# First layer of a graph network on one core: number row and angles in PSUM, both node sums in one bank, three queue orders changed

## The reference

```
rel_t = node_vec[src] - edge_weight
enc   = cos(rel_t * time_w + time_b)                 # 32 per edge
e     = concat(enc, edge_attr_64) @ We               # 96 -> 128
k, v  = (x@Wk+bk)[src] + e, (x@Wv+bv)[src] + e ;  q = (x@Wq+bq)[dst]
alpha = sum(q*k per head) / 8
a     = softmax of alpha over the edges of one dst
h     = layernorm(x + segment_sum(v*a, dst) + x@Wskip + bskip)
out   = layernorm(h + segment_sum(edge_weight*h[src], dst) @ W.T + b)   # second layer
```

## Time and profile before

| | us |
|---|---|
| median of 3 runs | 9845.34 (9844.81 to 9847.26) |
| profiled execution | 9864.48 |
| its span | 9862.8 |

### The profile page before, as it was taken

The page is one execution under the profiler, slowest core; times in us unless marked ns, Lnnn a source line. Parts: engine busy times, 40 slices in busy tenths (PEclk is TensorE's granted clock), DMA queues, the critical chain, the costliest instruction groups (busy, mean ns, idle before and its releaser), DMA issues.

```text
span 9862.8 us, 272152 instructions
## 1 busy us (share of the span) xinstructions
PE 7624.6 (77%) x52868; PEld 7101.3 (72%) x52869; DVE 8560.3 (87%) x21301; ACT 5115.0 (52%) x20838; POOL 6708.6 (68%) x6871
## 2 busy tenths in 40 slices
PE   6477777777777777777756777788888888888855
PEld 2477777777777777777756777787888877877754
DVE  5899999999999999999987666799999999999968
ACT  2377777777777777777753333333333333333300
POOL 0477777777777777777745777777777777777720
PEclk8688988888888888898875555688888888888888
DMA  6467666676666666666632222355555555555544
GB/s 191 114 180 178 179 177 177 178 179 178 176 177 180 177 176 177 178 181 177 177 97 69 71 71 71 106 151 147 149 147 149 148 148 149 148 148 149 148 133 116
DMA packets 1631706, 1484.67 MB, mean 151 GB/s; under 512 B 792007, under 2 KB 1363043, under 8 KB 1631203
## 3 DMA queue, kind: packets, MB, share of 16 engines
q1 hardware_dynamic: 1374244, 848.34, 34.3%
q0 software_dynamic: 257088, 632.95, 22.8%
HBM read 1225.51 MB, written 254.87 MB: 150 GB/s over the span
## 4 chain that ended last, share of the span: by engine, by line
issue 25%; DVE 19%; POOL 18%; PE 14%; DMA 7%; ACT 7%; DVEq 6%; SPq 3%; ACTq 2%; POOLq 0%
POOL message_scratch L869 17%; DMA message_scratch<-ohT,idx 6%; PE bank L982 3%; DVE y_all L1537 3%; PE bank L973 3%; ACT arena L1154 2%; DVEq L531 2%; PE bank L955 2%; PE bank L1015 2%; PE bank L963 2%; DVE acc L1670 1%; SPq L728 1%; DVE oh L1583 1%; DVE oh L1576 1%; DVE kve L1523 1%
## 5 line engine op out<-in xcount | busy, mean ns | idle before, releaser
L817 POOL DMA_INDIRECT kv<-kv_scratch,arena x3136 | 3265.7, 1041 | 1236.6 <-issue 837.5
L869 POOL DMA_INDIRECT message_scratch<-ohT,idx x3232 | 3214.2, 994 | 1079.0 <-issue 880.2
L1261 ACT ACTIVATE ohT<-bank,kv 128x128 f32<-128x128 f32 x3232 | 923.9, 369 | 2703.8 <-DMA message_scratch<-ohT,idx 2665.1
L1154 ACT ACTIVATE arena<-arena,weights 128x65 f32<-128x65 f32 x7040 | 1771.6, 337 | 2.4 <-PE bank L982 2.3
L1063 PE MATMUL bank<-acc,oh 128*128 x6464 | 1211.2, 345 | 520.3 <-ACT ohT L1262 514.4
L1063 PEld LDWEIGHTS bank<-acc,oh 128*128 128x128 f32 x6464 | 1054.7, 247 | 627.7 <-issue 625.2
L1077 PE MATMUL bank<-oh,kve 128*128 128x128 f32 x8640 | 1387.7, 321 | 144.7 <-DVE arena L1838 107.8
L982 PE MATMUL bank<-arena,oh 128*128 128x130 f32 x7040 | 1164.1, 318 | 280.8 <-DVE acc L1670 274.8
L1077 PEld LDWEIGHTS bank<-oh,kve 128*128 128x128 f32 x8640 | 1248.0, 227 | 167.8 <-issue 157.3
L982 PEld LDWEIGHTS bank<-arena,oh 128*128 128x128 f32 x7040 | 1048.2, 227 | 362.6 <-issue 295.1
L973 PE MATMUL bank<-arena,ohT 128*128 128x128 f32 x7040 | 1090.6, 306 | 0.0
(11 more groups left out here) (232 smaller groups left out, 12653.6 us busy)
## 6 DMA issues: line engine op xcount, KB each, us to landing
kve<-message_scratch SPq DMA_DIRECT2D x2160, 129.0 KB
kve<-nodes_scratch SPq DMA_DIRECT2D x880, 256.0 KB
feat<-in_edge_attr_dram SPq DMA_DIRECT2D x880, 96.0 KB
feat<-block_scratch SPq DMA_DIRECT2D x812, 98.0 KB
arena<-q_scratch SPq DMA_DIRECT2D x880, 64.0 KB
message_scratch<-ohT,idx POOLq DMA_INDIRECT x3232
kv<-kv_scratch,arena POOLq DMA_INDIRECT x3136
feat<-in_edge_attr_dram SPq DMA_DIRECT2D x880, 32.0 KB
```

Source lines behind the costliest of these rows:

```text
L817: pool.indirect_dma_start(kv[:, k, g, :], None, kv_d, bass.IndirectOffsetOnAxis(ap=group_rows[:, half, k * G + g, 0:1].bitcast(I32), axis= ...
L869: pool.indirect_dma_start(msg_d, bass.IndirectOffsetOnAxis(ap=idx[:, k, g:g + 1], axis=0), sum_ring[:, k % RING1, g, :], None).then_inc(s_ ...
L1154: op = act.activation(wv[:, st.k % 2, g, h, :], vR[:, st.k, g, h, :], ACT.Copy, scale=weights[:, st.k // ROUND, g, st.k % ROUND, h:h + 1])
L1261: act.activation(sum_ring[:, st.k % RING1, g, 0:C], banks[2 + st.k % 2][:, g * P:(g + 1) * P], ACT.Copy, scale=taken[:, st.k, g, 2:3])
```

## The change

- `agg_ps`: both node sums lie in bank 6, one beside the other. PE's `sum_stage` waits for `s_acc` of the step just before (it waited for that of two steps before).
- Bank 7 holds the number row, time_b and `turns`. DVE's L1503, L1506, L1508 and L1559 read or write them there. Two copies fill them once.
- PE's order in a body: feat, q, e, sum (it was feat, sum, q, e).
- ACT's order: arg first, of step k+17 (it was behind sine, of step k+18); then featc, weigh, sine, and the once-a-round stages. `EDGES` follows.
- DVE's order: the block number before ke; `sum_stage` behind ke and angle(2); `forward_stage` behind onehotT and `backward_stage` behind product.

```
-        turns = room(BATCH * G * TD).rearrange("p (b t) -> p b t", t=TD)
-        agg_ps = [banks[6 + j][:, 0:HEADS * HB] for j in range(2)]
+        agg_ps = [banks[6][:, j * HEADS * HB:(j + 1) * HEADS * HB] for j in range(2)]
+        brow_ps = banks[7][:, P:P + TD]
+        turns = banks[7][:, 2 * P:2 * P + BATCH * G * TD].rearrange("p (b t) -> p b t", t=TD)
 # PE sum_stage
-                wait(pe, s_acc, st.before(2))
+                wait(pe, s_acc, st.s)
 # PE body
-  at(i, k, (feat_stage, 15), (sum_stage, 1), (q_stage, 14), (e_stage, 15))
+  at(i, k, (feat_stage, 15), (q_stage, 14), (e_stage, 15), (sum_stage, 1))
 # ACT body
-            EDGES, group1 = {0: 6, 6: 8, 14: 2}, {}
+            EDGES, group1 = {0: 7, 7: 8, 15: 1}, {}
-  at(i, k, (featc_stage, 15), (weigh_stage, 2), *sines, (arg_stage, 18), *gaps, *exps, *smalls)
+  at(i, k, (arg_stage, 17), (featc_stage, 15), (weigh_stage, 2), *sines, *gaps, *exps, *smalls)
 # DVE, once, ahead of the pipeline
+            dve.tensor_copy(irow_ps, irow[:, :])
+            dve.tensor_copy(brow_ps, brow[:, :]).then_inc(s_tab, 1)
+            dve.wait_ge(s_tab, 3)
 # DVE angle(0): brow -> brow_ps; onehot_stage: irow -> irow_ps
 # DVE body
-  at(i, k, *turn[0], (ve_stage, 14), *turn[1], (ke_stage, 14), *turn[2], (block_stage, 0), *once(5, forward_stage),
-     (onehotT_stage, 15), *once(5, backward_stage), (product_stage, 13), *once(4, run_stage, first_stage),
+  at(i, k, *turn[0], (ve_stage, 14), *turn[1], (block_stage, 0), (ke_stage, 14), *turn[2], (sum_stage, 0),
+     (onehotT_stage, 15), *once(5, forward_stage), (product_stage, 13), *once(5, backward_stage), *once(4, run_stage, first_stage),
      ...
-     (sum_stage, 0), *once(8, pen_stage), *once(2, keep_part(0), keep_part(1), keep_part(2)))
+     *once(8, pen_stage), *once(2, keep_part(0), keep_part(1), keep_part(2)))
```

More of the change, by code:

```diff
@@ L1212, in body @@
                     if k in EDGES:
-                        groups_stage(mybir.EngineType.Activation, group1, Step(i, k + 18), EDGES[k])
+                        groups_stage(mybir.EngineType.Activation, group1, Step(i, k + 17), EDGES[k])
                     sines = [(sine_stage, 16)] if k % BATCH == 0 else []
@@ L1502, in stage_of @@
                     if n == 0:
-                        op = dve.tensor_tensor(a, a, brow[:, :].unsqueeze(1).to_broadcast([P, BATCH * G, TD]), ALU.add)
+                        op = dve.tensor_tensor(a, a, brow_ps.unsqueeze(1).to_broadcast([P, BATCH * G, TD]), ALU.add)
                     elif n == 1:
@@ L1558, in onehot_stage @@
                 wait(dve, s_agg, st.before(QS))
-                dve.tensor_tensor(oh[:, st.k % QS, :, :], irow[:, :].unsqueeze(1).to_broadcast([P, G, P]),
+                dve.tensor_tensor(oh[:, st.k % QS, :, :], irow_ps.unsqueeze(1).to_broadcast([P, G, P]),
                                   rel0[:, st.k // ROUND, st.k % ROUND, :].unsqueeze(2).to_broadcast([P, G, P]), ALU.is_equal).then_inc(s_oh, 1)
```

## The result

The changed kernel took 10321.9 us (median of 4 runs, 10305.9 to 10334.1) against 9846.3 us for the kernel before, now also over 4 runs: a ratio of 1.0478, 95% interval 1.0462 to 1.0493. It is slower by 476 us; I forecast slower by 320 us, with 10305 us as the upper end of the range. The profiled execution took 10305.9 us, its span is 10304.2 us.

What follows compares the result with a forecast made beforehand. DVE bounds the kernel, though not quite, waiting for ACT's products and PE's e. Terms 2.12 - 0.90 - 0.23 + 1.40 + 0.52 = +2.91 us a round, times 110 rounds: +320 us, 10165 us; range 9985 to 10305.

Steps and rivals of the forecast that it cites:

- ACT's new order: Body 6: table load, exp and dropx now precede ACT's products, which angle(0) awaits without slack; +1.74 us a round.
- "Cost 0" for the wait of PE's sum: PE's sum waiting for the sum just before is covered by ACT's idle time; 0, range -0.2 to +0.4 us a round.
- The write into PSUM: DVE's L1506 loses its fast mode with a PSUM destination: 130 ns, four times a round, +0.52 us.
- Reads from PSUM: DVE's L1559, L1503 and L1508 cost nothing more with a PSUM operand; range -0.01 to +0.08 us per instruction.
- Rival 2: PSUM reads cost DVE 0.08 us in each of 16 instructions a round: 141 us on top, 10305 us; chance 0.07.
- -0.90 for e: PE makes e before the node sum, so ve's waits for PE fall away: -0.90 us a round.
- +2.12 in body 6: DVE's angle(0) waits longer for ACT's products: 1.74 from exp plus 0.38 from DVE's earlier node sum, per round.
- +1.40 in body 4: Later backward scan delays PE's small results, ACT's copy and the products behind it; angle(0) waits +1.40 us a round.
- +0.38 for the node sum in front of new: DVE's node sum now precedes new, so the chain to body 6's products begins 0.38 us later.
- The small copy: In body 4 ACT's smallc, about 0.2 us, stands before the products and waits for PE; part of +1.40 us a round.
- Rival 1: Only the exp delay counts, body 4's backward-chain delay being taken up: 166 us more, 10010 us; chance 0.15.
- Rival 3: Faster: ACT runs a body ahead, PE's early e wins, only 0.52 us is paid: 9778 us; chance 0.08.

Runs made afterwards that it cites:

- the extra work: The changed kernel with PE forming two of the eight node sums of a round (steps 3 and 5) twice over, same result: 10223.8 us, ratio 1.0377.

## Why the prediction was right in kind and wrong in size

*ACT's new order* was the right cause. Undoing it gives back all (9847.5 us); alone it costs 208 us. Exp in front of the products with no slack, +1.74 us: the rows after show 1.75 us.

*"Cost 0" for the wait of PE's sum* held: two banks change nothing (10274.3 and 10269.5 us). *The write into PSUM*, 0.52 us a round or 57 us, measured 52. *Reads from PSUM*, 0: held. Rival 2 (reads from PSUM cost DVE) has fallen with that.

*-0.90 for e* held in the wait, and PE's order alone is worth even more in the kernel before, 143 us.

*The terms that were mis-sized: the two waits behind PE, in body 6 and in body 4.* The forecast had +2.12 in body 6, less 0.68 of ve, so +1.44; measured is +1.95. It had +1.40 in body 4; measured is +1.89. The step that failed is that I took PE's part of both chains as unchanged: I added only what ACT and DVE put in between, and took PE as ready when the backward scan ends.

The chains by their parts, means over all rounds of the stretch. From new_stage's start to angle(0) of body 6 it took 6.55 us before and takes 8.81 after: +2.26, where I had +1.74 for exp. Feat starts 2.12 us after new_stage's start before and 2.46 after, +0.34. ACT's copy starts behind feat's start 0.06 later than before. From the start of weigh to that of the products it took 1.92 us and takes 3.78: exp makes 1.75 of it, and the table load starts 2.03 us after weigh where the products started 1.92 after it, 0.11. In body 4 PE's small products start 1.60 us after the backward scan's start, 1.26 before, again +0.34; another 0.2 us is issue time between copy and products.

The two 0.34 are PE's clock. PE stands 9.0 us a round before (630 us in 70 rounds) and 11.5 after (737 in 64), and more of its work then runs at the granted 0.50. From newT's start to feat's the clock was 0.50 throughout in 22 of 70 rounds before, in 52 of 64 after, and in 5 of 65 with the extra work. The round of the earlier trace rows was one of the slow ones (newT 1.89 us; the fast ones have 1.06), so the rows of a single round could not tell how many there are. From alphaT's start to the small products' the mean clock is 1.00 before, 0.82 after, 0.97 with the extra work. The wait just in front does not tell it: PE stood 1.67 us before alphaT in the kernel before and stands 0.82 after. With the extra work feat starts 1.96 us after new and the small products 1.28 us after the scan's start, and the kernel gets 98 us faster, more than the two 0.34 (75 us). Some of this loss, then, the kernel before pays as well.

In sum, of the 156 us that the forecast lacked, the two delays on PE are 2 x 0.34 x 110 = 75 us, the issue time behind the copy 22, the 0.06 and 0.11 of body 6 19, L1654 (353 ns in place of the 188 of before) 18, body 0 (0.28 where I had 0.15) 14. The first is shown by runs, the others are only read from rows, and some 8 us stay open.

*+0.38 for the node sum in front of new* is not settled. With DVE's order alone body 6 waits less than before (1.34 us for 1.87). With PE's new order in place it waits more: 1.52 us in the changed kernel with ACT's old order, 0.68 with PE's order alone. The place of the node sum was not taken back by itself in the changed kernel.

*The small copy* was priced too low for the same reason: 361 us alone in the changed surroundings (I expected 175 to 210). PE's small products are late there, body 4 waits for them, and in all 65 rounds of the stretch newT then runs at the granted 0.50, so body 6 waits longer too.

*Terms don't add.* From the kernel before, ACT +208, DVE +65, write +52, PE -143 add up to +182; together they make +476. The surplus comes with ACT's order. Without its term the sum is -26 us, and the kernel without it has 9847.5 us, where the kernel before had 9844.0. ACT's order costs 208 us alone and 474 in the changed surroundings. There the small products start 1.71 us after the backward scan's start even with ACT's old order, yet body 4 waits 0, since the products stand in front of the copy. Behind the copy the same lateness is on the path. The scans' new places are 79 us of it.

*Rival 1* (body 4's delay is absorbed) is refuted: 1.89 us a round there. *Rival 3* (faster) has half a truth: in the kernel before, PE's order alone wins 143 us.

## What to carry to other kernels

Rotating a cyclic queue is free only if no once-in-a-while stage changes sides; look which stages pass each other, and whether the consumer of the delayed one has slack in that body. Read an engine's durations at the clock it will have after the change: where an added wait makes PE stand longer, take the slow rows of the trace for the upper end, and count over many rounds how often they come in place of reading one. The largest gain lay in none of the edits of waits or memory, but in two moves of PE's queue: nothing that waits for a late result in front of work that others wait for.

## What the runs showed of the hardware that I had not expected

A second, useless forming of two node sums per round made the kernel 98 and 173 us faster, with the granted clock going from 0.87 to 0.90 and from 0.85 to 0.93 in the stretch of 3000 us. And a small DVE instruction, L1654 with 16 elements, takes 353 ns behind the reduction of 512 elements (L1548), where it took 188 behind the node sum. In the ten other kernels with the node sum moved its mean is 242 to 356 ns, in the others 174 to 194. What causes it no run shows.
